# Decoder of twelve layers on one core: relu experts computed transposed, capacity experts fed by gathers

## The chip, the cores and the metric

The kernel runs on one core of a Trainium2 chip. The metric is the device time of one execution in microseconds. The compute engines are TensorE (PE, with PEld for its weight loads), VectorE (DVE), ScalarE (ACT) and GpSimd (POOL); SyncE (SP) issues DMAs. Each runs its own instruction stream and waits for the others on semaphores. A float32 matmul appears in the trace as two records.

## The reference, cut to what matters

A decoder of four blocks with three sublayers each works on x of 8 sequences x 256 tokens x 256 features (2,048 tokens). After every sublayer x becomes `layernorm(x + sublayer(x))`. Two of the twelve sublayers are touched.

The sixth, the relu experts:

```
sel_probs = sigmoid(x @ expert_sel.T)                 # 16 experts
_, sel_index = top_k(sel_probs, 4)
sel_val = take(sel_probs, sel_index); sel_val = sel_val / clip(sel_val.sum(-1), 1e-9) * route_scale
scores_all = relu(einsum('btd,edh->bteh', x, keys))   # 64 hidden values an expert
values_all = einsum('bteh,ehv->btev', scores_all, values)
out = sum over the 4 chosen experts of values_all * sel_val
```

The last, the capacity experts: each token goes to its likeliest of 8 experts, and an expert takes the first 320 of its tokens.

```
probs = softmax(tokens @ gate_w); expert_idx = argmax(probs)
pos = cumsum(one_hot(expert_idx), axis=0) - 1
sec_mask = mask1[:, :, None] * one_hot(pos, 320)
expert_input = einsum('tec,td->ecd', sec_mask, tokens)
expert_output = relu(expert_input @ w1) @ w2          # hidden size 1024
out = einsum('tec,ecd->td', probs[:, :, None] * sec_mask, expert_output)
```

## The kernel before

Each layer is a block of five instruction streams, and a new block starts when all engines have finished the last. x lives on the chip twice: `x_nat`, tokens on partitions in 16 tiles of 128, and `x_t`, features on partitions. The weights of layer k+1 are fetched while layer k runs. PSUM is split into `S.R` (two halves of two banks of 512 columns), `S.T` (two banks) and `S.O` (two banks). `keep_warm` (L209) issues matmuls of 512 columns whose result nobody reads, and `settle` takes a semaphore back to zero.

**Relu experts** (`moe_relu`, L2798). `pe_logits` (L2548) and `pe_logits_by_token` (L2560) produce the router's logits, which VectorE and ScalarE turn into a gate for each token and expert (L2913 to L2930, with `dve_top` at L2579). Then TensorE goes over the 8 sequences of 256 tokens. `hidden` (L2841) multiplies a tile of 128 tokens as the stationary side with the keys of all 1,024 hidden values as the moving side, in pieces of 512 columns. VectorE clips the 128x1024 result and multiplies it by the gates (L2938). `outputs` transposes `hid`, 8 blocks of 128 columns for each of two tiles (L2853); ScalarE copies them to `hid_t` (L2900); then come the products with the values (L2865). The tail of the sequence before (sum at L2945, LayerNorm at L103 to L127, transposes at L144, copy to `x_t` at L153) is done in between. Because the result overwrites `x_t`, SyncE copies the sequence's part of `x_t` to `xc` first (L186).

**Capacity experts** (`moe_capacity`, L3499). VectorE finds the expert and, with two TensorE products (L3601, L3602) and a scan, the rank of each token among its expert's tokens (L3759). From the rank it makes `to`, the slot of each token in a DRAM area of 8 x 320 rows that SyncE has filled with zeros (L3564). GpSimd scatters the 16 tiles of `x_nat` to it, one indirect DMA a tile (L3825). When all have landed, TensorE warms up (L3652) and SyncE loads the rows of the experts, 256 + 64 each, into `xe` (L3558, L3559), two experts at a time. For each expert TensorE transposes its rows (L3611), computes the first layer (L3628) with relu on ScalarE (L3678) and VectorE (L3778) in turn, transposes the rows of the next expert, and computes the second layer (L3645) over `ROWS`, two tiles of 128 slots and one of 64:

```
for t, n in ROWS:
    for f in range(FC):
        last = nc.tensor.matmul(S.O[0:n, t // 2, (t % 2) * D:(t % 2 + 1) * D], hid[:, f, t * P:t * P + n], w2[:, s, f, :],
                                start=(f == 0), stop=(f == FC - 1))
```

ScalarE copies the third tile out and stores it (L3688, L3690); VectorE copies the other two (L3785) and ScalarE stores them (L3693). SyncE loads the weights of the expert after next (L3552, L3553) when `ew_free` says that this one has finished. At the end GpSimd gathers every token's row (L3833), and VectorE and ScalarE finish the last LayerNorm.

Of the kernel before, what the change touches and what calls it, by code (L numbers as in the profile page):

```python
# [9 lines left out]
BF16 = mybir.dt.bfloat16  # L10
I32 = mybir.dt.int32
U32 = mybir.dt.uint32
# [4 lines left out]
P = 128  # L17
# [37 lines left out]
def columns(parts):  # L55

    at, out = 0, {}
    for name, n in parts:
# [7 lines left out]
                 ("head", HT), ("line_head", H), ("even", 1), ("odd", 1), ("sel", 3 * H)])  # L66
# [14 lines left out]
    columns([("keys", C * 1024), ("values", 8 * 256), ("sel", C * LOGITS), ("route_scale", 1)]),  # L81
# [2716 lines left out]
def moe_relu(nc, S, k):  # L2798

    W, TB = S.arena[k % 2], PACK[k]  # L2800
    E, EH, CHOSEN, NT = 16, 64, 4, B * TT
    HC = E * EH // P
    with ExitStack() as ctx:
# [7 lines left out]
        pick = sb("pick", [P, NT, CHOSEN, E])  # L2811
        gate = sb("gate", [P, NT, E])
        total = sb("total", [P, NT])
        hid = sb("hid", [P, TT, E * EH])
        hid_t = sb("hid_t", [P, HC, T])
        logits_t = sb("logits_t", [P, BANK])
        block = ctx.enter_context(nc.Block())

        @block.sync
        def _(sp):  # L2820
            sync_x(nc, S, sp, 0)
            prefetch(nc, S, sp, k + 1)
            with sp.Fori(1, B) as b:
                sync_x(nc, S, sp, b)
            sp.wait_ge(S.xc_free, 1)

        @block.tensor
        def _(pe):
            keys, values = part(W, TB, "keys", C), part(W, TB, "values", HC)
            x = S.xc[:, :, 1:1 + T]  # L2830
            pe.wait_ge(S.weights_ready[k], 16)

            def hidden():
                pe.wait_ge(S.xc_ready, 16)
                pe.sem_inc(S.xc_ready, -16)
                for tt in range(TT):
                    pe.wait_ge(S.r_free[tt], 1)
                    pe.sem_inc(S.r_free[tt], -1)
                    for at in (0, BANK):
                        for c in range(C):  # L2840
                            last = nc.tensor.matmul(S.R[:, tt, at:at + BANK], x[:, c, tt * P:(tt + 1) * P], keys[:, c, at:at + BANK],  # L2841
                                                    start=(c == 0), stop=(c == C - 1))
                    last.then_inc(S.h_full, 1)

            def outputs():
                for tt in range(TT):
                    pe.wait_ge(S.h_ready, 1)
                    pe.sem_inc(S.h_ready, -1)
                    for j in range(2):
                        pe.wait_ge(S.t_free[j], 1)  # L2850
                        pe.sem_inc(S.t_free[j], -1)
                        for i in range(4):
                            last = nc.tensor.transpose(S.T[:, j, i * P:(i + 1) * P], hid[:, tt, (4 * j + i) * P:(4 * j + i + 1) * P], S.ident)  # L2853
                        last.then_inc(S.at_full, 1)
                pe.wait_ge(S.t_free[0], 1)
                pe.sem_inc(S.t_free[0], -1)
                pe.wait_ge(S.t_free[1], 1)
                pe.sem_inc(S.t_free[1], -1)
                pe.sem_inc(S.t_free[0], 1)
                pe.sem_inc(S.t_free[1], 1)  # L2860
                pe.wait_ge(S.o_free[0], 1)
                pe.sem_inc(S.o_free[0], -1)
                for tt in range(TT):
                    for c in range(HC):
                        last = nc.tensor.matmul(S.O[:, 0, tt * D:(tt + 1) * D], hid_t[:, c, tt * P:(tt + 1) * P], values[:, c, :],  # L2865
                                                start=(c == 0), stop=(c == HC - 1))
                last.then_inc(S.y_full, 1)

            def tail():
                pe.wait_ge(S.o_free[1], 1)  # L2870
                pe.sem_inc(S.o_free[1], -1)
                tail_pe(nc, S, pe, 1)

            pe_logits(nc, S, pe, part(W, TB, "sel", C))
            pe_logits_by_token(nc, S, pe, logits_t)
            hidden()
            keep_warm(nc, S, S.T[:, 0, :], 8)
            outputs()

            with pe.Fori(0, B - 1):  # L2880
                hidden()
                tail()
                outputs()
            keep_warm(nc, S, S.T[:, 0, :], 4)
            tail()
            keep_warm(nc, S, S.T[:, 0, :], 2)

        @block.scalar
        def _(act):
            act_logits(nc, S, act, logits_t)  # L2890
            act.wait_ge(S.max_ready, 1)
            act.sem_inc(S.max_ready, -1)
            nc.scalar.activation(prob[:], prob[:], ACT.Exp, scale=-1.0).then_inc(S.p_ready, 1)

            def hidden_transposed():
                for tt in range(TT):
                    for j in range(2):
                        act.wait_ge(S.at_full, 1)
                        act.sem_inc(S.at_full, -1)
                        nc.scalar.activation(hid_t[:, 4 * j:4 * j + 4, tt * P:(tt + 1) * P],  # L2900
                                             S.T[:, j, :].rearrange("p (c t) -> p c t", c=4), ACT.Copy).then_inc(S.t_free[j], 1)

            with act.Fori(0, B) as b:
                hidden_transposed()
                tail_act(nc, S, act, 1, b)

        @block.vector
        def _(dve):
            dve.wait_ge(S.weights_ready[k], 16)
            each = [P, NT, E]  # L2910
# [10 lines left out]
            dve_top(nc, S, dve, gate, prob, top, index, index_f, pick, CHOSEN, E)  # L2921
            nc.vector.tensor_reduce(total[:], gate[:], AX.X, ALU.add)
            dve.drain()
            nc.vector.tensor_scalar(total[:], total[:], 1e-9, None, ALU.max)
            dve.drain()
            nc.vector.reciprocal(total[:], total[:])
            dve.drain()
            nc.vector.tensor_tensor(gate[:], gate[:], total[:].unsqueeze(2).to_broadcast(each), ALU.mult)
            dve.drain()
            nc.vector.tensor_scalar(gate[:], gate[:], part(W, TB, "route_scale"), None, ALU.mult)  # L2930
            dve.drain()
            with dve.Fori(0, B) as b:
                for tt in range(TT):
                    dve.wait_ge(S.h_full, 1)
                    dve.sem_inc(S.h_full, -1)
                    if tt == TT - 1:
                        dve.sem_inc(S.xc_free, 1)
                    nc.vector.scalar_tensor_tensor(hid[:, tt, :].rearrange("p (e h) -> p e h", e=E),  # L2938
                                                   S.R[:, tt, :].rearrange("p (e h) -> p e h", e=E), 0.0,
                                                   gate[:, bass.ds(b * TT + tt, 1), :].rearrange("p a e -> p (a e)").unsqueeze(2).to_broadcast([P, E, EH]),  # L2940
# [1158 lines left out]
```

## Time and profile before

| what | value |
|---|---|
| time, median of 3 runs | 3391.46 us (3388.67 to 3393.8) |
| the profiled execution: its own time, its span | 3394.49 us, 3392.7 us |
| TensorE matmul busy | 3077.6 us, 91% |
| VectorE, ScalarE, GpSimd busy | 1659.0 us (49%), 1222.0 us (36%), 291.9 us (9%) |
| mean granted TensorE clock | 0.967 |
| relu experts, first to last matmul | 2053.2 to 2229.5 us |
| capacity experts, first matmul to end of span | 3141.6 to 3392.7 us |

The busy shares are means over twelve layers of different kinds; what a layer's change is worth is read from its own stretch of the trace. A granted clock of 1.00 is 2.4 GHz, 0.50 is 1.2 GHz. In a timeline row stand the start, the length, the engine, the line, the operation and its operands, and in brackets the idle time of that engine before it with what ended it.

### The profile page before, as it was taken

How to read it: one execution, taken by the hardware profiler on the slowest of the kernel's cores; microseconds unless marked ns; L12 is line 12 of the kernel's file. 1: busy time of each engine (PE TensorE's matmuls, PEld its weight loads, DVE VectorE, ACT ScalarE, POOL GpSimd, SP SyncE). 2: the span in 40 equal slices, each digit the busy share in tenths (PEclk: the TensorE clock that was granted, in tenths of full speed). 3: DMA queues.
4: the chain of work that ended last, by engine and by line, in shares of the span. 5: the costliest groups of instructions: out<-in, count | busy, mean ns of one | idle time of the engine just before them, and what ended most of it. 6: DMA issues, size and time to landing. Idle time of an engine off the chain costs nothing. (4 is left out here: it accounts for less than half of the span.)

```text
span 3392.7 us, 56135 instructions
## 1 busy us (share of the span) xinstructions
PE 3077.6 (91%) x22954; PEld 1959.4 (58%) x22954; DVE 1659.0 (49%) x2939; ACT 1222.0 (36%) x2636; POOL 291.9 (9%) x511
## 2 busy tenths in 40 slices
PE   6999899999989998899999988989999899889695
PEld 3665566666658885556666655656655333346463
DVE  4665344444433234534444443225556999957112
ACT  1332244455431112235544441113323666623011
POOL 1111000000000000000000000000011000001102
PEclk9999999999999999799999999989999999989797
DMA  2001000000100002000000000000001000000432
GB/s 104 18 13 62 9 1 1 1 1 1 60 16 0 0 0 85 15 1 1 1 1 1 1 26 28 12 31 23 10 26 38 16 1 1 1 19 14 150 130 86
DMA packets 36410, 85.14 MB, mean 25 GB/s; under 512 B 3246, under 2 KB 30103, under 8 KB 32599
## 3 DMA queue, kind: packets, MB, share of 16 engines
q1 hardware_dynamic: 31831, 75.06, 6.3%
q0 software_dynamic: 1536, 4.20, 0.4%
q8 instruction: 170, 2.79, 0.3%
q10 hardware_dynamic: 2816, 2.62, 0.2%
q14 instruction: 57, 0.47, 0.0%
HBM read 53.90 MB, written 9.44 MB: 19 GB/s over the span
## 5 line engine op out<-in xcount | busy, mean ns | idle before, releaser
L2329 ACT ACTIVATE prob<-R,neg_max 128x333 f32<-128x333 f32 x512 | 268.8, 538 | 182.3 <-DVE neg_max L2399 182.3
L3420 DVE TENSOR_TENSOR_SCAN arena<-arena,u 128x512 f32<-128x512 f32 x256 | 289.5, 1201 | 0.1
L2399 DVE TENSOR_REDUCE neg_max<-R 128x2 f32<-128x666 f32 x256 | 205.6, 845 | 97.0 <-PE R L2209 97.0
L2220 PEld LDWEIGHTS T<-const,prob 128*128 128x128 f32 (+1 forms) x1536 | 183.3, 143 | 96.3 <-issue 66.2
L2405 DVE COPY prob_t<-T 128x384 f32<-128x384 f32 x256 | 141.6, 553 | 188.4 <-PE T L2220 183.2
L2220 PE MATMUL T<-const,prob 128*128 128x128 f32 (+1 forms) x1536 | 210.0, 273 | 19.7 <-DVE prob_t L2405 19.5
L2336 ACT ACTIVATE prob_t<-T 128x384 f32<-128x384 f32 x256 | 126.3, 493 | 213.2 <-PE T L2220 206.6
L3351 ACT ACTIVATE arena<-delta,neg_a 128x510 f32<-128x510 f32 x256 | 177.2, 717 | 46.7 <-DVE arena L3420 45.7
L2169 PE MATMUL O<-arena,keys_in 128*128 128x512 f32 (+1 forms) x384 | 183.8, 603 | 5.0 <-ACT arena L2310 2.4
L2164 PE MATMUL O<-keys_in,arena 128*128 128x333 f32 x512 | 170.3, 458 | 1.2 <-DVE arena L2380 1.2
L3257 PE MATMUL R<-arena,diag 64*64 64x512 f32 x1024 | 136.1, 622 | 24.6 <-DVE arena L3420 24.4
L2648 PE MATMUL R<-x_t,arena 128*128 (+1 forms) x640 | 150.7, 380 | 0.8 <-PEq L2644 0.2
L2512 POOL COPY rec_rows<-rec 128x256 f32<-128x256 f32 x128 | 51.4, 402 | 1001.2 <-DVE rec L2410 1001.2
L2648 PEld LDWEIGHTS R<-x_t,arena 128*128 128x128 f32 x640 | 120.6, 190 | 19.4 <-issue 3.0
L2158 PE MATMUL O<-keys_in,arena 128*128 128x256 f32 x512 | 124.5, 387 | 3.3 <-ACT keys_in L2304 2.4
L2657 PE MATMUL O<-arena,hid 128*128 128x256 f32 x512 | 120.9, 379 | 2.2 <-PEq L2654 2.2
L2180 PE MATMUL O<-arena,attn_t 128*128 128x256 f32 x512 | 117.4, 382 | 1.0 <-DVE ysb L2382 1.0
L2770 DVE SCALAR_TENSOR_TENSOR ysb<-O,gate_b,ysb 128x256 f32<-128x256 f32 x112 | 49.0, 479 | 140.9 <-DVEq L2767 140.9
L2416 DVE TENSOR_TENSOR attn_t<-O,arena 128x256 f32<-128x256 f32 x128 | 53.8, 421 | 129.9 <-ACT arena L2341 129.9
L2164 PEld LDWEIGHTS O<-keys_in,arena 128*128 128x128 f32 x512 | 88.2, 190 | 40.9 <-DVE arena L2380 7.4
L212 PE MATMUL R<-ctx_t,const 128*128 128x512 f32 x162 | 82.5, 639 | 29.1 <-DMA slots_in<-x_nat,to 26.4
L2657 PEld LDWEIGHTS O<-arena,hid 128*128 128x128 f32 x512 | 97.0, 190 | 16.0 <-issue 2.6
(463 smaller groups left out, 5488.1 us busy)
## 6 DMA issues: line engine op xcount, KB each, us to landing
w<-w_dram SPq DMA_DIRECT2D x16, 1024.0 KB, 7.1
arena<-pack_dram SPq DMA_DIRECT2D x2, 4100.0 KB, 15.0
q_pad<-q_pad SPq DMA_DIRECT2D x24, 224.0 KB, 2.7
arena<-pack_dram SPq DMA_DIRECT2D x4, 1284.0 KB, 6.0
arena<-pack_dram SPq DMA_DIRECT2D x1, 4896.0 KB, 15.3
arena<-k_nat SPq DMA_DIRECT2D x16, 224.0 KB, 2.7
arena<-arena SPq DMA_DIRECT2D x16, 224.0 KB, 2.8
arena<-pack_dram SPq DMA_DIRECT2D x1, 2707.0 KB, 14.8
```

The lines of the kernel that those rows point to most:

```text
L2164: last = nc.tensor.matmul(bank[:, 0:XK], wkv[:, c, i * P:(i + 1) * P], keys[:, c, :], start=(c == 0), stop=(c == C - 1))
L2169: last = nc.tensor.matmul(bank[0:n, :], keys[:, c, first:first + n], wkv[:, c, XI + i % 2 * BANK:XI + (i % 2 + 1) * BANK], start=(c == 0), ...
L2220: last = nc.tensor.transpose(S.T[0:n, i, kc * P:(kc + 1) * P], prob[:, g % 2, i, first:first + n], S.ident)
L2329: last = nc.scalar.activation(prob[:, g % 2, i, :], S.R[:, g % 2, i * BANK:i * BANK + XK], ACT.Exp, bias=neg_max[:, g % 2, i:i + 1], accum ...
L2336: nc.scalar.activation(prob_t[:, m % 2, 1, :, qt * P:(qt + 1) * P], S.T[:, 1, 0:3 * P].rearrange("p (c q) -> p c q", c=3), ACT.Copy).then_ ...
L2399: nc.vector.tensor_reduce(neg_max[:, g % 2, :], S.R[:, g % 2, :].rearrange("p (i n) -> p i n", i=2)[:, :, 0:XK], AX.X, ALU.max, negate=Tru ...
L2405: nc.vector.tensor_copy(prob_t[:, m % 2, 0, :, qt * P:(qt + 1) * P], S.T[:, 0, 0:3 * P].rearrange("p (c q) -> p c q", c=3)).then_inc(M.pt_ ...
L2648: last = nc.tensor.matmul(S.R[:, e % 2, f * T:(f + 1) * T], w[:, f * P:(f + 1) * P], S.x_t[:, c, bass.ds(b * T, T)], start=(c == 0), stop= ...
L2657: last = nc.tensor.matmul(S.O[:, slot, tt * D:(tt + 1) * D], src[:, f * T + tt * P:f * T + (tt + 1) * P], w[:, f, :], start=(f == 0), stop ...
L3257: last = nc.tensor.matmul(sums(i, a)[to:to + HB, :], diag[rows, i % CT, n + a, :], state[rows, (q + a) % HELD, :], start=(a == 1 and n == ...
L3351: nc.scalar.activation(decay[:, q % DEEP, :].rearrange("p (b t) -> p b t", b=PAIR)[:, :, 1:T], delta[:, i % 2, :].rearrange("p (b t) -> p ...
L3420: nc.vector.tensor_tensor_scan(state[:, q % HELD, :], decay[:, q % DEEP, :], u[:, i % 2, :], 0.0, ALU.mult, ALU.add)\
```

## The change

**Relu experts.** The hidden values are computed transposed: the keys are the stationary side (128 hidden values), 256 tokens of `x_t` the moving side, in four groups of two blocks. The gates must then vary over partitions. They are split into three bf16 parts whose sum is the float32 gate, transposed on TensorE once for all tokens (`gate_t`), and for each sequence spread over the hidden values by bf16 products with a 0/1 matrix `expand` that comes with the weights; ScalarE copies the spread gates to `gates`, VectorE clips and multiplies. The eight sequences are written out, with `outputs` one sequence and the tail two sequences behind. The result goes straight to `x_nat`, and `xc` is not used. The gates are made from `mask` and the normalised probabilities instead of by one multiplication for each rank.

**Capacity experts, dispatch.** x is stored to DRAM as it is. VectorE makes, for each token, its place within a tile of 128 slots (`at_place`, one-hot over 128 columns) and its token number under the expert and tile it belongs to (`at_tile`, 24 columns); TensorE's products of the two, summed over the 16 token tiles, give `holds`, the token number in every slot. GpSimd gathers the rows of each expert into `xe` with three indirect DMAs. An empty slot gathers token 0. There are 7 warm-up matmuls instead of 4, and they wait for no DMA.

**Capacity experts, third tile.** The 64-slot tile's second layer is computed in two halves of 128 output columns, one on PSUM partitions 0 to 63 and one on 64 to 127. ScalarE copies 128x128 values and stores them with two DMAs.

The diff, cut to its core:

```diff
@@ moe_relu, TensorE
+            def hidden(b, g):
+                if b >= 1:
+                    pe.wait_ge(M.exp_done, G * (b - 1) + g + 1)
+                for h in range(2):
+                    for c in range(C):
+                        last = nc.tensor.matmul(hidden_bank(g)[:, h * T:(h + 1) * T], keys[:, c, (2 * g + h) * P:(2 * g + h + 1) * P],
+                                                S.x_t[:, c, b * T:(b + 1) * T], start=(c == 0), stop=(c == C - 1))
+                last.then_inc(M.s_full, 1)
+
+            def spread(b, half):
+                if b >= 1 or half:
+                    pe.wait_ge(M.kg_ready, 2 * b + half)
+                for h in range(4):
+                    c = 4 * half + h
+                    last = nc.tensor.matmul(S.T[:, h // 2, h % 2 * T:(h % 2 + 1) * T], expand[:, c * P:(c + 1) * P],
+                                            gate_t[:, b * T:(b + 1) * T], start=True, stop=True)
+                last.then_inc(M.st_full, 1)
...
             pe_logits(nc, S, pe, part(W, TB, "sel", C))
+            hidden(0, 0)
             pe_logits_by_token(nc, S, pe, logits_t)
+            for g in range(1, G):
+                hidden(0, g)
+            keep_warm(nc, S, S.T[:, 1, :], 11)
+            settle(pe, M.setup, 1)
+            for j, bank in enumerate(banks):
+                for i in range(4):
+                    last = nc.tensor.transpose(bank[0:64, i * P:(i + 1) * P], gate_wide[:, 4 * j + i, :], S.ident)
+                last.then_inc(M.k_full, 1)
+            settle(pe, M.k_sb, len(banks))
+            for i in range(B + 2):
+                if i < B:
+                    spread(i, 0)
+                    for g in range(G):
+                        if i >= 1:
+                            hidden(i, g)
+                        if g == 1:
+                            spread(i, 1)
+                if 0 <= i - 1 < B:
+                    if i == B:
+                        keep_warm(nc, S, hidden_bank(0), 2)
+                    outputs(i - 1)
+                if 0 <= i - 2 < B:
+                    if i == B + 1:
+                        keep_warm(nc, S, hidden_bank(0), 7)
+                    transposed(i - 2)
+            keep_warm(nc, S, hidden_bank(0), 2)
@@ moe_relu, ScalarE
+            def spread(b, half):
+                act.wait_ge(M.st_full, 2 * b + half + 1)
+                if b >= 1:
+                    act.wait_ge(M.exp_done, G * (b - 1) + 2 * half + 2)
+                nc.scalar.activation(gates[:, half, :, :], S.T[:], ACT.Copy).then_inc(M.kg_ready, 1)
@@ moe_relu, VectorE
+            def clipped(b, g):
+                dve.wait_ge(M.s_full, G * b + g + 1)
+                dve.wait_ge(M.kg_ready, 2 * b + g // 2 + 1)
+                nc.vector.scalar_tensor_tensor(hid[:, b % 2, 2 * g:2 * g + 2, :].rearrange("p c t -> p (c t)"), hidden_bank(g), 0.0,
+                                               gates[:, g // 2, g % 2, :], ALU.max, ALU.mult).then_inc(M.exp_done, 1)
@@ moe_capacity, SyncE
+            sp.dma_start(S.xe_dram[0:N, :].rearrange("(t p) d -> p t d", p=P), S.x_nat[:]).then_inc(S.scattered, 16)
+            for s in range(2):
+                weights(s, s)
...
+            for e in range(E3):
+                s = e % 2
+                if e >= 2:
+                    sp.wait_ge(S.ew_free[s], 1)
+                    sp.sem_inc(S.ew_free[s], -1)
+                    weights(e, s)
+                sp.wait_ge(S.fetched[s], 48 * (e // 2 + 1))
+                sp.sem_inc(S.xe_ready[s], 1)
@@ moe_capacity, TensorE
+            for half in range(2):
+                pe.wait_ge(S.h_ready, 1)
...
+                for tt in range(half * NT // 2, (half + 1) * NT // 2):
+                    last = nc.tensor.matmul(S.O[:, 0, 0:3 * E3], at_place[:, tt, :], at_tile[:, tt, :, :].rearrange("p e k -> p (e k)"),
+                                            start=(tt == 0), stop=(tt == NT - 1))
+            last.then_inc(S.v_full, 1)
...
-                for t, n in ROWS:
+                for t in range(2):
                     for f in range(FC):
-                        last = nc.tensor.matmul(S.O[0:n, t // 2, (t % 2) * D:(t % 2 + 1) * D], hid[:, f, t * P:t * P + n], w2[:, s, f, :],
+                        last = nc.tensor.matmul(S.O[:, 0, t * D:(t + 1) * D], hid[:, f, t * P:(t + 1) * P], w2[:, s, f, :],
                                                 start=(f == 0), stop=(f == FC - 1))
+                last.then_inc(S.y_full, 1)
+                for f in range(FC):
+                    for h in range(2):
+                        last = nc.tensor.matmul(S.O[h * HB:(h + 1) * HB, 1, 0:P], hid[:, f, 2 * P:CAP], w2[:, s, f, h * P:(h + 1) * P],
+                                                start=(f == 0), stop=(f == FC - 1), skip_group_check=True)
                 last.then_inc(S.v_full_act, 1)
 
-            pe.wait_ge(S.scattered, 16 * NT)
-            keep_warm(nc, S, S.R[:, 0, 0:BANK], 4)
+            keep_warm(nc, S, S.R[:, 0, 0:BANK], 7)
@@ moe_capacity, GpSimd
-            for tt in range(NT):
-                nc.gpsimd.indirect_dma_start(S.xe_dram[:, :], bass.IndirectOffsetOnAxis(ap=to[:, tt:tt + 1], axis=0),
-                                             S.x_nat[:, tt, :], None).then_inc(S.scattered, 16)
+            for e in range(E3):
+                s = e % 2
+                pool.wait_ge(S.xe_free[s], 1)
+                pool.sem_inc(S.xe_free[s], -1)
+                for t, n in ROWS:
+                    nc.gpsimd.indirect_dma_start(xe[0:n, s, t, :], None, S.xe_dram[0:N, :],
+                                                 bass.IndirectOffsetOnAxis(ap=holds[0:n, 3 * e + t:3 * e + t + 1], axis=0)).then_inc(S.fetched[s], 16)
```

## Rows read from the trace of the kernel before

**Rows 1.** The page's first line.

```profile
span 3392.7 us, 56135 instructions
```

**Rows 2.** Stretches: engines' busy time, granted clock (PEclk), DMA share, GB/s.

```profile
core 0: us, PE busy (x) PEld busy (x) DVE busy (x) ACT busy (x) POOL busy (x), PEclk, DMA share, GB/s
2078.20:2088.30 10.10, 10.00 (x32) 8.34 (x33) 0.00 (x0) 0.00 (x0) 0.00 (x0) 0.69 0.01 2
2088.30:2107.30 19.00, 16.98 (x71) 11.49 (x71) 4.96 (x10) 2.66 (x5) 1.55 (x3) 1.00 0.04 14
...
3149.00:3175.30 26.30, 0.01 (x1) 0.01 (x1) 3.05 (x14) 0.00 (x0) 15.69 (x16) 0.50 0.67 256
```

**Rows 3.** Timeline of the relu stage, first microseconds.

```profile
2056.14 0.63 PE L2560 MATMUL O<-const,logits_t 128*128 128x128 f32 x4 [1.04 <-PEq L2558]
...
2064.14 0.23 DVE L2588 CAST index_f<-index 128x128 f32<-128x128 uint32 x1
...
2071.80 1.23 DVE L2938 SCALAR_TENSOR_TENSOR hid<-R,gate 128x1024 f32<-128x1024 f32 x1 [0.44 <-DVEq L2935]
...
2078.30 10.19 PE L2865 MATMUL O<-arena,hid_t 128*128 128x256 f32 x32 [1.32 <-PEq L2862]
```

**Rows 4.** Timeline of the relu stage, sequences 1 and 7.

```profile
2088.33 7.03 PE L2841 MATMUL R<-arena,xc 128*128 128x512 f32 x16
...
2088.74 0.69 DVE L2945 TENSOR_TENSOR ysb<-O,x_nat 128x512 f32<-128x512 f32 x1 [14.05 <-DVEq L2944]
...
2099.83 7.14 PE L2865 MATMUL O<-arena,hid_t 128*128 128x256 f32 x32 [1.41 <-PEq L2862]
...
2202.24 7.03 PE L2841 MATMUL R<-arena,xc 128*128 128x512 f32 x16
```

**Rows 5.** Timeline of the relu stage, its end.

```profile
2213.67 8.83 PE L2865 MATMUL O<-arena,hid_t 128*128 128x256 f32 x32 [1.34 <-PEq L2862]
...
2227.62 1.88 PE L212 MATMUL T<-ctx_t,const 128*128 128x512 f32 x4
```

**Rows 6.** Timeline of the capacity stage up to the first transposes.

```profile
3150.99 0.28 DVE L3759 TENSOR_REDUCE rank<-ranks 128x16 f32<-128x128 f32 x1
...
3153.54 1.24 POOL L3825 DMA_INDIRECT slots_in<-x_nat,to  x1 [10.80 <-POOLq L3823]
...
3172.85 0.96 POOL L3825 DMA_INDIRECT slots_in<-x_nat,to  x1 [0.30 <-issue]
3175.30 6.09 PE L212 MATMUL R<-ctx_t,const 128*128 128x512 f32 x8 [26.42 <-DMA slots_in<-x_nat,to]
...
3181.23 1.16 PE L3611 MATMUL T<-const,xe 128*128 128x128 f32 x6
```

**Rows 7.** Timeline of the capacity stage, experts 0 to 2.

```profile
3194.28 10.74 PE L3645 MATMUL O<-w,hid 128*128 128x256 f32 x48 [0.74 <-PEq L3642]
3204.95 8.88 PE L3628 MATMUL R<-xe_t,w 128*128 128x320 f32 x32
...
3205.93 0.60 ACTq L3690 DMA_DIRECT2D slots_out<-ye  x1
...
3207.50 0.71 ACT L3678 ACTIVATE hid<-R 128x640 f32<-128x640 f32 x1 [1.82 <-ACTq L3677]
...
3226.23 8.88 PE L3628 MATMUL R<-xe_t,w 128*128 128x320 f32 x32
```

**Rows 8.** Groups by form, and one timeline row of the perceiver (L2235).

```profile
1997.28 1.52 PE L2235 MATMUL O<-prob_t,v 128*64 128x256 f32 x12
...
L716 PE MATMUL R<-masks,ident_b 128*128 128x256 bf16 x64 | 10.6, 292 | 0.0
...
L2310 ACT ACTIVATE arena<-O 128x512 f32<-128x512 f32 x32 | 19.1, 598 | 52.8 <-PE O L2169 52.8
...
L3645 PEld LDWEIGHTS O<-w,hid 128*64 128x64 f32 x125 | 16.5, 137 | 11.2 <-issue 2.7
```

**Rows 9.** DMA issues: KB each, median us from issue to landing.

```profile
x_nat<-x_dram SPq DMA_DIRECT2D x1, 2048.0 KB, 20.3
...
arena<-slots_out,back POOLq DMA_INDIRECT x16, 2.8
```

More of the change, by code:

```diff
@@ L80 @@
     columns(_XATT),
-    columns([("keys", C * 1024), ("values", 8 * 256), ("sel", C * LOGITS), ("route_scale", 1)]),
+    columns([("keys", C * 1024), ("values", 8 * 256), ("sel", C * LOGITS), ("route_scale", 1), ("expand", 8 * P)]),
     columns(_MHA),
@@ L2829, in _ @@
             keys, values = part(W, TB, "keys", C), part(W, TB, "values", HC)
[L2830 to L2862, printed above, removed]
+            def hidden(b, g):
[6 more added lines that the diff above has]
+                last.then_inc(M.s_full, 1)
@@ new lines, in transposed @@
+            def transposed(b):
+                act.wait_ge(M.yt_full, b + 1)
+                nc.scalar.activation(S.x_t[:, :, b * T:(b + 1) * T], S.O[:, 1, :].rearrange("p (c t) -> p c t", c=C), ACT.Copy)\
+                    .then_inc(M.xt_done, 1)
+            for i in range(B + 2):
+                if i < B:
+                    spread(i, 0)
+                    spread(i, 1)
+                if 0 <= i - 2 < B:
+                    transposed(i - 2)
+            settle(act, M.st_full, 2 * B)
@@ new lines, in result @@
+            def result(b):
+                dve.wait_ge(M.y_full, b + 1)
+                nc.vector.tensor_tensor(ysb[:, b % 2, :, :], S.O[:, 0, :].rearrange("p (t d) -> p t d", t=TT),
+                                        S.x_nat[:, b * TT:(b + 1) * TT, :], ALU.add).then_inc(M.y_read, 1)
+                dve.drain()
+                for tt in range(TT):
+                    nc.vector.bn_stats(bst[:, tt, :], ysb[:, b % 2, tt, :])
+                dve.drain()
+                for tt in range(TT):
+                    last = nc.vector.bn_aggr(mv[:, b % 2, tt, :], bst[:, tt, :])
+                last.then_inc(M.ln_stat, 1)
@@ L3760, in _ @@
             dve.drain()
+            nc.vector.tensor_scalar(part_of[:], rank[:], float(P), None, ALU.is_gt)
             nc.vector.tensor_scalar(kept[:], rank[:], float(CAP), None, ALU.is_le)
+            dve.drain()
+            nc.vector.scalar_tensor_tensor(part_of[:], rank[:], 2.0 * P, part_of[:], ALU.is_gt, ALU.add)
+            nc.vector.tensor_tensor(token[:], token[:], kept[:], ALU.mult)
+            dve.drain()
+            nc.vector.scalar_tensor_tensor(place[:], part_of[:], -float(P), rank[:], ALU.mult, ALU.add)
@@ L3762, in _ @@
+            for half in range(2):
+                tiles, some = slice(half * NT // 2, (half + 1) * NT // 2), [P, NT // 2, P]
+                nc.vector.tensor_tensor(at_place[:, tiles, :], part(S.const, CONST, "count").unsqueeze(1).to_broadcast(some),
+                                        place[:, tiles].unsqueeze(2).to_broadcast(some), ALU.is_equal)
+                dve.drain().then_inc(S.h_ready, 1)
             nc.vector.scalar_tensor_tensor(slot_f[:], from_end[:], -float(CAP), rank[:], ALU.mult, ALU.add)
+            nc.vector.tensor_tensor(gates[:], total[:], kept[:], ALU.mult)
```

257 lines of the change are left out of this document (146 added, 111 removed).

## The prediction

> **What bounds the kernel now.** I read the page first for the span [rows 1], then the table of stretches for the two stages that the diff touches, with the granted TensorE clock [rows 2], then the timeline inside them [rows 3 to 7]. The other ten stages keep their code, so only these two stretches can move.
>
> In the relu stage TensorE sets the pace. In the stretch of one sequence it is busy 16.98 of 19.00 us at a granted clock of 1.00, that is 2.4 GHz; VectorE has 4.96 us of work, ScalarE 2.66 [rows 2]. The first products of sequence 1 start at 2088.33 and those of sequence 7 at 2202.24, six periods of 18.98 us [rows 4]. Of a period 6.83 us are key products (16 records, 0.427 us apart, as the eight in the row that covers 7.03), 7.14 the value products [rows 4]; what is left, about 5 us, is the 16 transposes of `hid`, 4 of the tail, the waits for ScalarE's copies between them, and some time at 1.2 GHz: the same 32 value records take 7.14 us in one sequence, 8.83 in the last, 10.19 in the first [rows 3 to 5].
>
> In the capacity stage nothing runs on TensorE from 3149 to 3175.3: 0.01 us busy in 26.3 [rows 2]. GpSimd issues 16 scatters, 3153.54 to 3173.81, 1.27 to 1.29 us apart; TensorE's warm-up starts at 3175.30 and the first transposes at 3181.23 [rows 6]. After that TensorE is again the bound: one expert per 21.28 us (3204.95 to 3226.23), of which 10.74 are 48 records of the second layer, 0.22 us apart, the last 16 of them the 64-row tile [rows 7].
>
> **Relu stage: the loop.** The new order computes the hidden values already transposed (keys stationary, tokens moving). It removes the 16 transposes of `hid`, ScalarE's copies between them and the waits on both. Key products become 32 records of 256 columns, the form of the value products, so 32 x 0.213 = 6.8 us (7.14 less the last one's tail) [rows 4], the same as now. Added is the spread of the gates: 8 bf16 products of 256 columns. A 256-column bf16 record has mean 292 ns and is one record [rows 8]; a float32 product of that size is two records: 0.107 us apart, 0.85 in all. Value products stay 6.83, the tail's four transposes 0.45 (four in 0.63 including the last one's tail [rows 3]). Sum 6.83 + 0.85 + 6.83 + 0.45 = 14.96, against 18.98: 4.0 us a period.
>
> Nothing should stop TensorE: each wait is for work of at least half a period ago. VectorE per sequence: four products-with-gates of 512 elements at 0.69 (as the 512-element addition [rows 4]) instead of two of 1.23 [rows 3], so 2.8, with the rest about 5.3 us. ScalarE: two copies of 1,024 elements, each under twice 0.60 [rows 8], call it 1.03, and one of 512: 2.7 us. Both are below 15. GpSimd loses a copy that nobody waited for.
>
> **Relu stage: start and end.** Hidden group 0 now goes before the transposes of the logits, so the gate chain starts 0.6 us late. From the cast at 2064.14 [rows 3] the chain loses four multiplications and gains the three-way bf16 split; step by step I get the same end, 2071.3, plus 0.6: 2071.9. Today the first product with gates follows at 2071.80. New behind it: 16 transposes (1.7 us) with four ScalarE copies of 512 (0.60, overlapping) to 2074.8; spread, copy of 1.03, spread, copy, to 2078.3, when the products of sequence 1 can start. From there, at 2.4 GHz: first period without a tail 14.5, six of 14.96, then 2 warm-up products 1.7, the last values 6.83, one tail 0.45, 7 warm-ups 5.97, last tail 0.45, 2 warm-ups 1.7: 2078.3 + 14.5 + 89.8 + 17.1 = 2199.7. The LayerNorm chain of the last sequence (about 4.3 us) lies inside the 7 warm-ups. I add 4 us for the clock: the pause at the start takes it down, as it does now (granted 0.69 in the stretch 2078.2 to 2088.3 [rows 2]), which costs the 3.2 us between 10.19 and about 7.0, and one further dip of the kind seen in the last sequence. 2203.7 against 2229.5 today (2227.62 + 1.88 [rows 5]): **26 us**, bounds 22 (two more dips) and 30 (none).
>
> **Capacity stage: the dispatch.** The scatters and the reload of rows go; in their place a table of token numbers. From the rank (ends 3151.27 [rows 6]) five dependent short steps, at most 0.35 each as the rank's own 0.28 plus a drain, then 384 products (0.5, by elements from the 1,024 in 1.23 us [rows 3]) and 1,024 comparisons, 1.23: first half at 3154.5, second at 3155.8. TensorE: two halves of 16 records with 128x128 weights. At 2.4 GHz such records follow at 0.11 us [rows 3], at 1.2 twice that; the granted clock there is 0.50 [rows 2], so 6.8 us: 3161.4 (at the full clock 3157.6). Copy and handover, as long as now to the first scatter: 1.2, first gather at 3162.5. Gathers issue like scatters, 1.27 apart, three for expert 0, and the third lands 2.8 us after its issue [rows 9]: 3162.5 + 2.5 + 2.8 = 3167.8. Beside it run 7 warm-ups from 3161.4: 6.0 us at 2.4 GHz, 8.1 if the first third is still at 1.2 as today [rows 6]. First transposes at about 3168.8 instead of 3181.23: **12.4 us**, bounds 8 (landing delayed) and 15. The plain store of the 2 MB of x, issued at 3141.7, must be over by 3161.5; the 2 MB load at the kernel's start, in a crowd, took 20.3 us [rows 9], so even that bound hardly shows. The later gathers have a whole expert of time. SyncE now passes on "rows are there" behind its wait for the old expert's weights, which ends about 7 us before TensorE asks.
>
> **Capacity stage: the third tile.** 16 records of 256 columns become 32 of 128, alternating between the two column halves. Where the trace has such pairs, 12 records of 256 columns take 1.52 us [rows 8], 0.104 apart instead of 0.213: they run two at a time. The floor is 16 x 0.107 = 1.7 us, the ceiling no gain, 32 x 0.107 = 3.4. Weight loads are now as frequent as 0.053 us, for half the columns of the 0.11 above; nearest the pairs, I take 1.9. Saved 1.5 x 8 = **12 us**, bounds 0 and 13.6.
>
> The Trainium skill speaks against it (TensorE: Matmul & The Clock Gate, "What overlaps and what doesn't"): a weight load overlaps a running matmul only if its row group differs, and here both halves use all rows. Today's loads of that form, all rows too, cost nothing beside the matmuls (rival two has their rows). By the rule alone no record could be shorter than its own load, and the sum would be 20 us worse.
>
> ScalarE issues one more store per expert, 0.60 us [rows 7]. Its first relu, 0.71 us from 3207.50, then starts some 0.5 us later; TensorE writes that bank again only after 16 of the 32 first-layer records that cover 8.88 us from 3204.95, at 3209.2 [rows 7]. So it is hidden with 0.5 us to spare, except behind the last expert: +0.5. The longer constant costs +0.2 at the start.
>
> **Sum.** 26 + 12.4 + 12 - 0.7 = 49.7. The profiled execution took 3394.5 us (span 3392.7 [rows 1]), so 3344.8; it lies 3.0 above the median of 3391.5, so the median should be **3342 us**.
>
> **Rivals.**
> - The halves of the third tile don't overlap: 3354 (12%). For it: no row has 128-column pairs. Against: the 256-column ones.
> - A weight load can't be hidden there: at the 0.137 us that a 64-column load lasts on average [rows 8] 32 records take 4.4 us, a loss of 1.0 per expert instead of 1.5 gained: 3362 (3%). Against it: today these loads hide entirely under records 0.22 us apart [rows 7]. The page's rule above would give this case.
> - The relu loop waits or loses clock in several sequences, 1.7 us each time as in the last one [rows 5], say six times: 3352 (10%).
> - The first gathers queue behind weights still loading, 5 us: 3347 (8%).
> - Slower than before: after the pause at 2072 to 2078 TensorE never regains 2.4 GHz in the relu loop. Eight periods of 15 us become 30: +120, net 3462. It decides once more than 50 of the 120 us of work run at 1.2 GHz. Against it: the same pause is over within 10 us today, with the next stretch at 1.00 [rows 2] (2%).
> - The table comes no sooner than the scatters and the transposed form saves nothing: about 3380 to 3391 (1%).
>
> The forecast itself has 64%. Range 3329 to 3358: it takes in serial halves and the lost clock, leaves out the load-bound tile and the slower case. Faster 0.97, same 0.01, slower 0.02; 0.2% is about what a measurement of this kernel can tell from no change.
>
> **What would show it.** Relu: periods of 15.0 us, TensorE without idle time in them, granted clock 1.00, next stage near 2204. Capacity: first gather at 3162 minus 26, transposes six us later, experts 19.8 us apart, third tile 1.9 us. Wrong if the periods exceed 16, the experts 21, or if gathers of later experts hold up transposes.

## The result, and the profile after

The changed kernel takes 3348.4 us, median of four runs (3342.4 to 3349.6), against 3392.0 before: 43.7 us less, ratio 0.9869 (95% interval 0.9852 to 0.9886). In two later comparisons the ratio was 0.9876 (0.9861 to 0.9890) and 0.9867 (0.9849 to 0.9885). The forecast was 3342, with a range of 3329 to 3358. The profiled execution of the changed kernel was the quickest of the four, 3342.4 us with a span of 3340.6.

First the stage that the forecast had most wrong. The timeline of the changed kernel from the gates to the first values of the relu stage:

```profile
2049.72 1.92 PE L2548 MATMUL T<-x_t,arena 128*32 128x512 f32 x16 [0.59 <-PEq L2104]
...
2068.68 1.03 PE L2892 MATMUL T<-const,gate_wide 128*64 128x128 f32 x8
...
2073.21 0.61 PE L2858 MATMUL T<-gate_t,expand 64*128 64x256 bf16 x4 [1.12 <-ACT gates L2933]
...
2074.93 1.03 PE L2858 MATMUL T<-gate_t,expand 64*128 64x256 bf16 x4 [1.12 <-ACT gates L2933]
...
2075.90 6.01 PE L2849 MATMUL R<-x_t,arena 128*128 128x256 f32 x16
...
2082.38 3.72 PE L2849 MATMUL R<-x_t,arena 128*128 128x256 f32 x16
...
2085.94 7.07 PE L2868 MATMUL O<-arena,hid 128*128 128x256 f32 x32
```

L2858 are the products that spread the gates, L2849 the key products, L2868 the value products. The idle time in brackets, twice 1.12 us behind ScalarE's copies, is the pause that the forecast had seen. It takes the clock down: the same 16 records cover 6.01 us before 2082 and 3.72 after. This is the counterpart of the 10.19 us in [rows 3]. The table of stretches shows the same, and then a loop that never pauses (the columns are those of [rows 2]):

```profile
2072.00:2083.00 11.00, 8.77 (x32) 6.20 (x32) 3.96 (x6) 3.58 (x4) 0.00 (x0) 0.69 0.01 1
2083.00:2098.00 15.00, 15.00 (x73) 12.31 (x72) 4.59 (x10) 1.76 (x3) 0.93 (x2) 1.00 0.00 1
...
2158.00:2173.00 15.00, 15.00 (x74) 12.45 (x73) 5.02 (x11) 2.36 (x3) 0.53 (x1) 1.00 0.00 0
```

TensorE is busy 15.00 of 15.00 us at a granted clock of 1.00, where it was 16.98 of 19.00 [rows 2]. In the six other stretches up to 2204 it is busy throughout as well, at 1.00. One period, sequence 7, and the end of the stage:

```profile
2171.02 0.60 PE L2878 MATMUL O<-const,x_nat 128*128 128x128 f32 x4
2171.55 0.61 PE L2858 MATMUL T<-gate_t,expand 64*128 64x256 bf16 x4
...
2172.09 3.72 PE L2849 MATMUL R<-x_t,arena 128*128 128x256 f32 x16
...
2175.74 0.61 PE L2858 MATMUL T<-gate_t,expand 64*128 64x256 bf16 x4
...
2176.28 3.72 PE L2849 MATMUL R<-x_t,arena 128*128 128x256 f32 x16
...
2179.84 7.07 PE L2868 MATMUL O<-arena,hid 128*128 128x256 f32 x32
...
2186.74 0.60 PE L2878 MATMUL O<-const,x_nat 128*128 128x128 f32 x4
...
2202.69 1.88 PE L212 MATMUL R<-ctx_t,const 128*128 128x512 f32 x4
```

From transposes (L2878) to transposes a period has, start to start, 0.53 + 0.54 + 3.65 + 0.54 + 3.56 + 6.90 = 15.72 us: not 18.98 as in [rows 4] and not 14.96 as forecast. The stage ends at 2204.57 (2202.69 + 1.88), forecast 2203.7. That near hit is partly luck: the whole stage started 3.45 us earlier than before.

The capacity stage, in rows that answer to [rows 6] and [rows 7]:

```profile
3123.58 0.28 DVE L3857 TENSOR_REDUCE rank<-ranks 128x16 f32<-128x128 f32 x1
...
3125.73 2.56 DVE L3875 TENSOR_TENSOR arena<-const,place 128x1024 f32<-128x1024 f32 x2
...
3127.27 6.99 PE L3697 MATMUL O<-at_tile,arena 128*128 128x24 f32 x32 [5.81 <-PEq L3695]
...
3134.09 8.54 PE L212 MATMUL R<-ctx_t,const 128*128 128x512 f32 x14
...
3135.66 1.23 POOL L3944 DMA_INDIRECT xe<-slots_in,holds  x1 [20.65 <-POOLq L3942]
...
3142.47 1.16 PE L3708 MATMUL T<-const,xe 128*128 128x128 f32 x6
...
3162.59 1.97 PE L3747 MATMUL O<-w,hid 128*64 128x128 f32 x32
3164.49 8.88 PE L3725 MATMUL R<-xe_t,w 128*128 128x320 f32 x32
...
3184.19 8.85 PE L3725 MATMUL R<-xe_t,w 128*128 128x320 f32 x32
```

The table's 32 records take 6.99 us, as priced for 1.2 GHz. L3875 are the comparisons that make `at_place`, L3697 the products of the table, L3944 the gathers. The first gather goes out 12.1 us after the rank's start, where the first scatter went out 2.6 us after it, but three gathers are enough for expert 0. The transposes start at 3142.47, 11.9 us sooner by the stage's own clock. The third tile takes 1.97 us (forecast 1.9), and two experts follow at 19.56 and 19.70 us instead of 21.28.

All executions profiled in this study, cut at the same instructions, are the best view of where time goes. "Ahead" is the start of the relu stage's logits products; "relu" runs from there to the next layer's first product (L683); "between" to the capacity stage's logits products; "dispatch" to the first transposes of rows; "experts" to the last copy of a third tile; "end" to the end of the span.

| kernel | ahead | relu | between | dispatch | experts | end |
|---|---|---|---|---|---|---|
| before | 2053.2 | 176.6 | 911.8 | 39.6 | 173.1 | 38.3 |
| changed | 2049.7 | 155.2 | 909.9 | 27.7 | 159.6 | 38.5 |
| relu_only | 2057.7 | 155.3 | 910.1 | 38.8 | 173.3 | 38.1 |
| gather_only | 2052.2 | 170.2 | 914.2 | 28.5 | 173.4 | 37.9 |
| half_only | 2058.4 | 170.1 | 914.5 | 39.6 | 160.1 | 38.6 |
| after_again | 2061.8 | 155.1 | 910.1 | 27.6 | 161.7 | 38.7 |
| spread_128rows | 2060.9 | 149.7 | 911.2 | 28.6 | 161.7 | 38.5 |
| spread_f32 | 2061.4 | 179.1 | 911.6 | 28.6 | 159.7 | 38.6 |
| halves_in_turn | 2065.1 | 155.2 | 910.1 | 27.6 | 172.5 | 38.5 |
| all_three | 2059.7 | 149.1 | 911.4 | 26.6 | 159.8 | 38.5 |
| combined | 2058.8 | 145.0 | 909.0 | 24.2 | 159.9 | 38.7 |
| after_beside | 2051.0 | 155.7 | 906.9 | 27.8 | 161.7 | 38.6 |

Read the columns, not the rows. "Ahead" and "between" are the same code in every line, and spread over 15.4 and 7.6 us. The new relu stage gives 155.1 to 155.7 in five executions, the old one 170.1, 170.2 and 176.6. So the difference of the first two lines, 52 us of span, is 21.5 + 11.9 + 13.5 us in the changed stages less 0.2 at the end, and 5.4 us in stretches whose code is the same: 3.5 ahead and 1.9 between. The 3.5 are within what that column varies. Whether the 1.9 are too is open: all nine kernels with a new relu stage have 906.9 to 911.6 there, the three with the old one 911.8 to 914.5.

"Experts" has a variation of its own: 159.6 to 160.1 in five lines with the new tile in alternation, 161.7 in three. In those three the first layer of expert 0 covers 10.54 us instead of 8.85, and the other experts are as fast as in the changed kernel.

### The profile page after: what moved, and what is told of

Read it like the earlier page. It is cut to its first block and busy times, and to the rows that moved or that the text cites. A ratio compares the mean times of both kernels' runs of the same rounds, so it can differ in the third digit from the quotient of the medians.

```text
span 3340.6 us, 56267 instructions
## 1 busy us (share of the span) xinstructions
PE 3064.4 (92%) x23216; PEld 1976.1 (59%) x23216; DVE 1664.0 (50%) x2963; ACT 1219.3 (36%) x2624; POOL 292.1 (9%) x511
## 5 line engine op out<-in xcount | busy, mean ns | idle before, releaser
L2164 PE MATMUL O<-keys_in,arena 128*128 128x333 f32 x512 | 170.2, 458 | 1.2 <-DVE arena L2380 1.2
L3350 PE MATMUL R<-arena,diag 64*64 64x512 f32 x1024 | 136.0, 621 | 24.3 <-DVE arena L3513 24.2
L2164 PEld LDWEIGHTS O<-keys_in,arena 128*128 128x128 f32 x512 | 88.2, 190 | 40.9 <-DVE arena L2380 7.5
L2158 PEld LDWEIGHTS O<-keys_in,arena 128*128 128x128 f32 x512 | 92.2, 189 | 22.0 <-ACT q_t L2307 4.2
## 6 DMA issues: line engine op xcount, KB each, us to landing
arena<-pack_dram SPq DMA_DIRECT2D x2, 4100.0 KB, 15.4
```

The costliest lines, as they stand in the source:

```text
L2158: last = nc.tensor.matmul(bank[:, h * T:(h + 1) * T], wq[:, c, (2 * i + h) * P:(2 * i + h + 1) * P], keys[:, c, CTX:XK], start=(c == 0), s ...
L2164: last = nc.tensor.matmul(bank[:, 0:XK], wkv[:, c, i * P:(i + 1) * P], keys[:, c, :], start=(c == 0), stop=(c == C - 1))
L3350: last = nc.tensor.matmul(sums(i, a)[to:to + HB, :], diag[rows, i % CT, n + a, :], state[rows, (q + a) % HELD, :], start=(a == 1 and n == ...
```

## The experiments

Each kernel was run beside the kernel before; ratios are to it, over four to six executions. Only the two kernels that change the spread (spread_128rows and spread_f32) were executed once each, and of them only the stages are used.

**The three parts alone.** Kernel relu_only has the relu stage of the changed kernel and the capacity stage of the one before. Gather_only has the old relu stage and the new dispatch, with the old third tile. Half_only puts only this into the kernel before, with its copy and stores:

```diff
-                for t, n in ROWS:
+                for t in range(2):
...
+                for f in range(FC):
+                    for h in range(2):
+                        last = nc.tensor.matmul(S.O[h * HB:(h + 1) * HB, 1, 0:P], hid[:, f, 2 * P:CAP], w2[:, s, f, h * P:(h + 1) * P],
```

> The relu stage of the changed kernel with the capacity stage of the kernel before. From the stages of the two traces: first logits product of the relu stage to the first product of the next layer takes 176.6 us before and 155.2 after, so this kernel should be 21 to 22 us faster than before (ratio 0.9937). The forecast had put 26 us here. If the three parts helped each other, or if the missing microseconds of the whole lay in later layers, it would be nearer to 16 or to 26.

Measured: 0.9944 (0.9926 to 0.9963), 19 us. The stage itself is 155.3 us.

> The slot table and the gathers alone, old relu stage, old 64-row tile. From the traces, first logits product of the capacity stage to the first transposes: 39.6 us before, 27.8 after. So 12 us faster (ratio 0.9965). Rival: the later gathers, one expert ahead, cost something once the tile is the old one: under 9.

Measured: 0.9961 (0.9948 to 0.9973), 13 us; dispatch 28.5 us, experts 173.4 as before. The later gathers cost nothing.

> The halved third tile alone on the kernel before. 32 records in 1.97 us where 16 took 3.4 to 3.6: 1.7 us an expert, 13.5 in all, less 0.4 for the additional store behind the last expert: 13 us faster (ratio 0.9961). Rival, no overlap of the halves: no gain.

Measured: 0.9959 (0.9946 to 0.9972), 14 us; experts 160.1 us against 173.1.

> The changed kernel unedited, on this chip beside its parts. If the parts add, the time is before less 21.5, 12 and 13, that is 46.5 us faster (ratio 0.986). The first measurement gave 0.9869 with a profiled execution 6 us below the other three; rival: that execution was lucky and a typical one loses 6 us in TensorE clock, which would show as a span of 3346 and a granted clock of 0.970.

Measured: 0.9876 (0.9861 to 0.9890), 42 us by the ratio. The three parts give 46 together, within their intervals of about 6, 4 and 4 us: they add. The rival on the lucky execution was half right. This execution took 3355.0 us of span, 14.4 more than the first, but its mean granted clock is 0.972 against 0.973. The table says where: 12.0 us ahead of the relu stage, 2.1 in the experts. What made the 12.0 is open.

Half_only also shows what the forecast's base had been worth. First two more batches of value products of the kernel before, from the timeline of its relu stage, then the first ones of half_only, to be held against the 10.19 us of [rows 3]:

```profile
2118.22 8.83 PE L2865 MATMUL O<-arena,hid_t 128*128 128x256 f32 x32 [1.32 <-PEq L2862]
...
2193.57 8.83 PE L2865 MATMUL O<-arena,hid_t 128*128 128x256 f32 x32 [1.37 <-PEq L2862]
```

```profile
2083.51 7.14 PE L2865 MATMUL O<-arena,hid_t 128*128 128x256 f32 x32 [1.32 <-PEq L2862]
```

The same code behind the same pause runs 3 us faster here. Of the eight batches of value products one took 10.19 us in the kernel before and three took 8.83; in half_only, and in gather_only, one took 8.83 and seven 7.14. Their mean period over sequences 1 to 7 is 18.7 us instead of 18.98. The execution that was profiled before had met more of the 1.2 GHz level: from 2053 to 2090 its granted clock was 0.86, in the two others 0.95.

**Why a period takes 15.7 us and not 15.0.** Weight loads of the changed kernel in sequence 7, from the timeline of the loads:

```profile
2171.55 0.33 PEld L2858 LDWEIGHTS T<-gate_t,expand 64*128 64x128 bf16 x4 [0.17 <-issue]
2172.09 3.32 PEld L2849 LDWEIGHTS R<-x_t,arena 128*128 128x128 f32 x16 [0.21 <-issue]
2175.74 0.33 PEld L2858 LDWEIGHTS T<-gate_t,expand 64*128 64x128 bf16 x4 [0.33 <-issue]
2176.28 3.32 PEld L2849 LDWEIGHTS R<-x_t,arena 128*128 128x128 f32 x16 [0.21 <-issue]
2179.62 1.49 PEld L2868 LDWEIGHTS O<-arena,hid 128*128 128x128 f32 x7
```

The loads of value weights at 2179.62 start 0.22 us ahead of their matmul at 2179.84: they go in under the last key product. The loads of the spread start at 2171.55 and 2175.74, at the same time as their first matmuls. They had not gone in ahead. Two things differ at this boundary, the type (float32 to bf16) and the rows (128 to 64). One kernel changes the rows only, the other the type only:

```diff
# spread_128rows
-        expand = sb("expand", [64, HC * P], BF16)
-        gate_t = sb("gate_t", [64, N], BF16)
+        expand = sb("expand", [P, HC * P], BF16)
+        gate_t = sb("gate_t", [P, N], BF16)
...
+            nc.vector.memset(gate_t[64:P, :], 0.0)
# spread_f32
-        expand = sb("expand", [64, HC * P], BF16)
-        gate_t = sb("gate_t", [64, N], BF16)
+        expand = sb("expand", [64, HC * P])
+        gate_t = sb("gate_t", [64, N])
```

> The bf16 products that spread the gates get 128 rows instead of 64, the added ones zero; nothing else changes. In the changed kernel each batch of four loses about 0.33 us: 0.22 before its first weight load, 0.11 behind its last product, twice a sequence, so that a period of the relu loop is 15.72 us where the forecast had 14.96. If the loss comes from the change of the row count (64 after 128), the periods here are 15.1 us. If it comes from the change between float32 and bf16, they stay at 15.7.

> The same spread in float32, with 64 rows: eight records of 256 columns, 0.213 us apart, for four of 0.107, so 1.28 us more a batch. If the type change was the loss, it is gone: periods 15.72 - 0.66 + 2.56 = 17.6 us. If the row count was, it stays: 18.3 us. If both are innocent and the semaphore waits are the cause, 18.3 too, and the other kernel stays at 15.7.

Measured: with 128 rows the period is 15.13 us (value products at 2125.02, 2140.15, 2155.28) and the relu stage 149.7 instead of 155.1. Its loads:

```profile
2132.26 0.42 PEld L2858 LDWEIGHTS T<-gate_t,expand 128*128 128x128 bf16 x4
2132.69 3.33 PEld L2849 LDWEIGHTS R<-x_t,arena 128*128 128x128 f32 x16
2136.04 0.53 PEld L2858 LDWEIGHTS T<-gate_t,expand 128*128 128x128 bf16 x4
```

and the first matmul of the second batch:

```profile
2136.26 0.60 PE L2858 MATMUL T<-gate_t,expand 128*128 128x256 bf16 x4
```

Its load, at 2136.04, is 0.22 us ahead again, although it is bf16 after float32. Start to start, the transposes take 0.44 us instead of 0.53, a batch 0.43 instead of 0.54, and the two halves of the key products 3.46 instead of 3.65 and 3.56: 0.59 us a period. In float32 with 64 rows the gap stays:

```profile
2136.02 1.59 PEld L2858 LDWEIGHTS T<-gate_t,expand 64*128 64x128 f32 x8 [0.33 <-issue]
2137.94 3.32 PEld L2849 LDWEIGHTS R<-x_t,arena 128*128 128x128 f32 x16 [0.33 <-issue]
```

Its value products are 18.49 us apart (2141.50 to 2159.99), near the 18.3 of the row theory and far from 17.6. So it is the row count: here weights of 64 rows are not loaded under a running matmul of 128 rows, and the way back costs too (the loads of the keys at 2172.09 and 2176.28 start with their matmuls as well). The Trainium skill (TensorE: Matmul & The Clock Gate, "What overlaps and what doesn't") has loads overlap only where the row group differs. For equal rows these runs disagree: such loads start 0.22 us ahead. Rows 0 to 63 in the wake of rows 0 to 127 share rows with them, and those loads don't go ahead. Groups with no row in common were not tried.

**Do the halves of the third tile run together?**

```diff
-                for f in range(FC):
-                    for h in range(2):
+                for h in range(2):
+                    for f in range(FC):
```

> The third tile's 32 records ordered by half: first all for partitions 0 to 63, then all for 64 to 127, instead of alternating. The arithmetic is the same. If the gain of the halved tile comes from two neighbours in different column halves running at once, it is gone: tile 3.4 us or more instead of 1.97, expert 21.1 us instead of 19.6, 11 to 12 us slower than the changed kernel (about 32 us faster than before, ratio 0.990). If records of 64 columns by 128 are simply cheap, the tile stays at 2.0 and the time at that of the changed kernel.

Measured: the tile takes 3.33 us instead of 1.97, and experts 172.5 us in all:

```profile
3193.93 7.15 PE L3742 MATMUL O<-w,hid 128*128 128x256 f32 x32 [0.90 <-PEq L3739]
3201.01 3.33 PE L3747 MATMUL O<-w,hid 128*64 128x128 f32 x32
3204.27 8.88 PE L3725 MATMUL R<-xe_t,w 128*128 128x320 f32 x32
```

That is 12.9 more than in the changed kernel, but expert 0 met the long first layer of 10.54 us here; against the three lines of 161.7, which met it too, it is 10.8. From the second layer's start to the next expert's first product pass 10.67 us before [rows 7] (3194.28 to 3204.95), 10.34 here (3193.93 to 3204.27) and 8.98 in the changed kernel (3155.51 to 3164.49). So of 1.69 us an expert 1.36 come from neighbours in different column halves, and 0.33 stay when the halves go in turn. Where those 0.33 come from was not tested. The ratio over the runs, 0.9892 (0.9876 to 0.9907), shows less, 5 us against after_again, which ran on another chip, with overlapping intervals. The stage's own length is the sharper measure here.

**Warm-ups.** Three edits to the changed kernel. Starts of pauses are filled, two batches behind which nobody waits are cut:

```diff
# start of the relu loop
+            pe.wait_ge(M.k_sb, 2)
+            keep_warm(nc, S, S.T[:, 0, :], 1)
             settle(pe, M.k_sb, len(banks))
...
                     spread(i, 0)
+                    if i < 1:
+                        keep_warm(nc, S, S.O[:, 0, :], 1)
...
                             spread(i, 1)
+                            if i < 1:
+                                keep_warm(nc, S, S.O[:, 0, :], 1)
# its end
-                    if i == B:
-                        keep_warm(nc, S, hidden_bank(0), 2)
...
-                        keep_warm(nc, S, hidden_bank(0), 7)
+                        keep_warm(nc, S, hidden_bank(0), 4)
# capacity stage, ahead of the table's products and behind them
+            keep_warm(nc, S, S.R[:, 0, 0:BANK], 6)
...
-            keep_warm(nc, S, S.R[:, 0, 0:BANK], 7)
+            keep_warm(nc, S, S.R[:, 0, 0:BANK], 8)
```

> The changed kernel with three edits to its warm-ups. (1) Start of the relu loop: three single warm-up matmuls in the waits for ScalarE's copies. If they keep the clock at 2.4 GHz, the key products of sequence 1 take 3.7 us in their first half instead of 6.0: minus 2 us. (2) End of the relu stage: the two warm-ups ahead of the last value products go, the seven ahead of the last transposes become four: minus 1.7 and 2.5, so 4.2 us. (3) Capacity stage: six warm-ups while VectorE makes the table's operands, eight instead of seven behind it. If they hold the clock, the table's 32 records take 3.5 us of TensorE instead of 6.99, its end is then set by VectorE's second half, and the first transposes come 4 to 5 us earlier. Together 10 to 12 us below the changed kernel, 55 us below before: ratio 0.984 (0.9835 if the clock holds everywhere). Rival: warm-ups in a pause give nothing, as the clock falls anyway: only the 4.2 us of (2), ratio 0.986.

Measured: 0.9847 (0.9829 to 0.9866). By that it lies 7 to 10 us below the changed kernel as the three comparisons have it, with intervals that overlap theirs; the stages tell more. In the relu stage both edits help, 149.1 instead of 155.1 us: the first value products start 2.7 us sooner in the stage (2 expected), and 3.4 us come at the end (4.2 expected). In the timeline the pause is filled and the first key products take 3.72 us:

```profile
2083.74 1.13 PE L212 MATMUL O<-ctx_t,const 128*128 128x512 f32 x2
...
2085.46 3.72 PE L2849 MATMUL R<-x_t,arena 128*128 128x256 f32 x16
```

In the capacity stage only 1.2 of the 4 to 5 us came. The clock was already down when the warm-ups began. Of their twelve records the first five are 0.85 us apart and the last six 0.43; together they took 7.58 us and held up the table, whose own records then were quick:

```profile
3127.20 7.58 PE L212 MATMUL R<-ctx_t,const 128*128 128x512 f32 x12
...
3134.61 3.65 PE L3702 MATMUL O<-at_tile,arena 128*128 128x24 f32 x32
3138.10 8.81 PE L212 MATMUL R<-ctx_t,const 128*128 128x512 f32 x16
```

The granted clock of these stretches, from the table of stretches:

```profile
3128.00:3132.00 4.00, 4.00 (x6) 1.68 (x5) 3.38 (x14) 0.00 (x0) 0.00 (x0) 0.53 0.98 406
3132.00:3138.00 6.00, 6.00 (x39) 4.53 (x37) 2.56 (x5) 0.00 (x0) 0.00 (x0) 1.00 0.98 413
```

Of the 3.3 us that the table won, 1.9 were lost by starting it late: 14.4 us after the stage's first product (3120.19) instead of 12.5. Its operands had been there since 3132.90. The last kernel has four and seven warm-ups there, and the spread on 128 rows:

```diff
-            keep_warm(nc, S, S.R[:, 0, 0:BANK], 6)
+            keep_warm(nc, S, S.R[:, 0, 0:BANK], 4)
...
-            keep_warm(nc, S, S.R[:, 0, 0:BANK], 8)
+            keep_warm(nc, S, S.R[:, 0, 0:BANK], 7)
```

> The warm-up edits of the run before, with the spread on 128 rows, and in the capacity stage four warm-ups ahead of the table instead of six and seven behind it instead of eight. By the stages read so far: relu stage 149.1 less 5.4, so 143.7 us (155.1 in the changed kernel); from the capacity stage's first product to the first transposes 26.6 less 1.5 to 2, so 24.8 (27.7); experts as they are. 14 us below the changed kernel, 58 below before: ratio 0.983. Rival for the capacity part: with only four warm-ups the clock is still at 1.2 GHz when the table's products start, they take up to 7 us, and the transposes come no earlier than in the changed kernel.

> The changed kernel once more, on the chip of the combined one, for a comparison without a second chip in it. Relu stage 155.1 us and dispatch 27.6 to 27.7 again, as in both traces so far; the layers before the relu stage, whose code nobody changed, anywhere from 2050 to 2065 us. Ratio to before 0.987, 14 us above the combined kernel.

Measured: combined 3329.4 us, ratio 0.9809 (0.9789 to 0.9828); the changed kernel beside it 3346.8, ratio 0.9867 (0.9849 to 0.9885). The combined kernel beats both, by 17 us and by 62.5. Its relu stage takes 145.0 us (143.7 expected) and its dispatch 24.2 (24.8); in after_beside they take 155.7 and 27.8. From its timeline:

```profile
3119.81 5.84 PE L212 MATMUL R<-ctx_t,const 128*128 128x512 f32 x8
3125.83 3.72 PE L3703 MATMUL O<-at_tile,arena 128*128 128x24 f32 x32 [0.18 <-PEq L3701]
```

Eight records last 5.84 us, again five of them 0.85 us apart, and end 0.15 us after the operands are there (3125.50), and the table is at the full clock. Against the changed kernel beside it the two stages account for 10.6 + 3.6 us; another 1.8 is the long first layer of after_beside's expert 0, and the rest of the 17 is within what untouched code varies.

## Why the prediction was right

The mechanisms were right, each in its place, but for one cost that the forecast had at nothing, and the sum of the three terms, 50 us, stands against 46 from the parts measured alone and 42 to 45 from the whole, by its three ratios.

- **The relu loop.** The step "the sum 6.83 + 0.85 + 6.83 + 0.45 = 14.96" was mis-sized. The records are nearly right, and nothing waits for another engine, but the forecast had every weight load hidden, and around the 64-row batches they are not. A batch of gates costs 0.54 us, not 0.43, and its neighbours lose time too: 0.59 us a period, 5.4 us a stage by spread_128rows. The other 0.17 of a period are records a little longer than priced, 6.90 for the value products instead of 6.83 and 3.46 for each half of the key products instead of 3.42.
- **The base of that term.** 18.98 us a period was the mean of one execution. Two others of the same code take 170.1 and 170.2 us for the stage instead of 176.6. The 26 us were 21.5 against the profiled execution and 15 against the other two; relu_only, timed, gave 19. The base is not the larger part of the miss against that 19: of the 7 us, 5.4 are the loads.
- **The start of the loop.** The mechanism came as worked out: the pause behind ScalarE's copies takes the clock down and costs 2.3 us (6.01 against 3.72). In all_three, with the pause filled, the first value products start 2.7 us sooner. The products of sequence 1 started 26.2 us into the stage; the forecast had 25.1 (2078.3 less 2053.2). Of its 4 us for the clock only these 2.3 came, for the further dip did not: that and the 1.1 us partly cancel.
- **The dispatch.** 12.4 forecast, 11.9 in the profile, 13 alone. The table was priced at 1.2 GHz, 6.8 us, and took 6.99. The first gather came 12.1 us after the rank; the forecast had 11.5. Weights, store and gathers did not get in each other's way: the 2 MB of x landed in 8.3 us, at 3123.0, the last weights at 3133.1, and the first gather went out at 3135.7.
- **The third tile.** 12 forecast, 13.5 in the profile. 1.97 us a tile was as forecast (1.9), and about 0.2 us an expert more was won than counted, because the old tile cost 3.6 us to the next product (10.67 less 7.08 for the two full tiles) and not 3.4. Halves_in_turn shows that the pairing is four fifths of the gain.
- **The end.** 0.5 forecast; from the last copy of a third tile to the first gather of the output 4.8 us passed instead of 4.4, and the column "end" grew by 0.2. The 0.2 for the longer constant can't be seen beside the 15.4 us that "ahead" varies.
- **The slower rival**, a clock that stays down, had nothing to it: 1.00 from 2083 on. The load-bound tile did not come true either, but loads that are not hidden did: at the gates, where the row count changes.

That the time of the profiled execution, 3342.4, meets the forecast of 3342 to the microsecond is chance. The forecast was for a median, and that is 6 us higher.

## What to carry to other kernels

Cut several executions at the same instructions before trusting one as the base: here untouched code ranged over 15 us, as much as each part was worth. Put small products on as many rows as their neighbours have, zeros included, when they sit between large ones; here it cost VectorE 0.91 us once, to clear the added rows, and let their weights go in ahead. The warm-ups paid here where they filled a pause from its start, or ended when the work they were for was ready: when the clock was already down their first five records took twice as long, and four warm-ups ahead of the table with seven behind it did better than six and eight.

## What the hardware showed that had not been expected

- Weights of 64 rows did not load ahead under a matmul of 128 rows, nor the other way round. In bf16 that cost 0.59 us for two batches, gone with 128 rows; in float32 with 64 rows it stayed, 0.8 us by an estimate (18.49 less 15.13 less 2 x 1.28).
- 32 records of 64 columns by 128, alternating between column halves, took 1.97 us; in turn 3.33. Loads of 64 columns, 0.137 us each here too, kept pace with records 0.055 us apart.
- The plain 2 MB store of x in rows of 1 KB, ahead of 4 MB of weights on the same queue, landed in 8.3 us, as the DMA issues of the changed kernel show for the stretch 3114 to 3145 (KB, us to landing); the forecast had only the 20.3 us of [rows 9] as a bound.

```profile
w<-w_dram SPq DMA_DIRECT2D x4, 1024.0 KB, 11.7
slots_in<-x_nat SPq DMA_DIRECT2D x1, 2048.0 KB, 8.3
```
